# Spreading products of a decoder kernel put on 64 rows of TensorE each, instead of 128

## The chip, the cores and the metric

The kernel runs on one core of one Trainium2 chip. The metric is the device time of one execution in microseconds, as the median of several runs; lower is better. Each engine of the core (TensorE, VectorE, ScalarE, GpSimd, SyncE) runs its own list of instructions in order, and waits on semaphores that the others raise.

## The reference

Six sublayers of a pre-norm decoder are computed on 64 sequences of 128 tokens with 256 channels, each added to the running x. Two of them are attention layers with 16 heads of 16 channels and a softmax over all 128 keys; the mask of keys is in the first alone:

```python
x = x + _L0_attn_ref(_layernorm(x), ...)                       # attention in a window of 7 tokens
x = x + _L0_xattn_ref(_layernorm(x), ctx, ctx, mask, Wp, bp)   # tag "b" in the kernel
x = x + _L0_ffn_ref(_layernorm(x), ...)                        # slots and a gated unit
x = x + _L1_attn_ref(_layernorm(x), ...)                       # causal, with a position bias, tag "1"
x = x + _L1_xattn_ref(_layernorm(x), ctx, ...)                 # tag "x"
x = x + _L1_ffn_ref(_layernorm(x), ...)                        # quantized, with a convolution, tag "g"

# in _L0_xattn_ref
score = jnp.einsum('bhqd,bhkd->bhqk', q, k) / jnp.sqrt(jnp.float32(DK))
score = jnp.where(sm == 0, jnp.float32(-1000000000.0), score)
p_attn = jax.nn.softmax(score, axis=-1) * sm
# in _L1_xattn_ref
scores = jnp.einsum('bhqd,bhkd->bhqk', q, k)
attn = jax.nn.softmax(scores, axis=-1)
```

## The kernel before

The 64 sequences are worked on two at a time (B = 2). Four such pairs are in work at once: they are the four chains, and each chain has two of the eight PSUM banks (`c.ps[:, 0, :]` and `c.ps[:, 1, :]`, 128 partitions of 512 float32 each) and its own tiles in SBUF. A chain makes eight turns, each of them all six sublayers for two sequences, so there are 32 turns of a chain in all. What is interleaved with what is written out by hand: the strings in `ORDER` say for each engine from which chain its next step comes, a step being the code up to the next `yield`. These strings are the lists, and they are the same before and after the change.

Scores are made in two ways in the attention layers "b" and "x". First `scores` (line 1202) makes them with queries on the partitions, for one of two sequences and one half of the heads at a time, and VectorE takes the maximum over the keys (line 696). GpSimd splits each maximum into three bfloat16 parts (`split_pool`, into the tile `m3`), TensorE turns these over (line 1244), and ScalarE copies them to the tile `mT` (line 1004). Then `softmax_tensor` makes the scores a second time, with keys on the partitions (line 1258), and in the same PSUM bank a product ahead of them (line 1254) adds the maxima: its weights `pick` hold ones in the three rows of one head group, 32 rows of the partitions to each group, and zeros elsewhere, so that it spreads the maxima of that group over all 128 keys. ScalarE takes the exponential out of the banks (line 1013), and TensorE multiplies it with the values (line 1221).

In "b" the maxima must leave masked keys out. For this `scores` puts another product ahead of its own (line 1208), whose weights `first` are ones in one row and zero elsewhere, and whose other operand is the tile `mask_bf`, which holds the mask of the keys (0 or -2^30) in the same way on all 128 partitions.

The products of the scores themselves (lines 1212 and 1258) contract over 64 rows: rows 0 to 63 go to bank 0, rows 64 to 127 to bank 1, four products of 256 columns for each bank, and the two banks by turns. The products at lines 1208 and 1254 contract over all 128 rows, one product of 512 columns for each bank. Index `2 * i + o` of `pick` has its ones in rows 32 * (2 * i + o) to 32 * (2 * i + o) + 2, so for bank 0 they lie in rows 0 to 63 and for bank 1 in rows 64 to 127. A pair of these products is issued 256 times at line 1254 (32 turns of a chain, two layers, four each) and 128 times at line 1208 (32 turns, one layer, four each). Line 1317 uses `pick` as well, on 128 rows, and isn't touched.

Of the kernel before, what the change touches and what calls it, by code (L numbers as in the profile page):

```python
# [14 lines left out]
NSEQ, T, D = 64, 128, 256  # L15
# [16 lines left out]
GROUPS = 4  # L32
PER = H // GROUPS
# [166 lines left out]
def spread(ap, dim, n):  # L200
    ap = ap.unsqueeze(dim)
    shape = list(ap.shape)
    shape[dim] = n
    return ap.broadcast_to(shape)
# [423 lines left out]
def flat(tile):  # L628

    inner = " ".join("abcde"[:len(tile.shape) - 1])  # L630
    return tile.rearrange(f"p {inner} -> p ({inner})")
# [570 lines left out]
def scores(e, c, k, v, masked=False):  # L1202

    t, b, x = c.t, v // 2, v % 2
    mm = [None, None]
    if masked:
        for i in range(2):
            e.matmul(c.ps[:, i, :], k["first"][:], spread(t["mask_bf"][:, T * b:T * b + T], 1, PER), start=True, stop=False)
    for j in range(KT):
        for i in range(2):  # L1210
            p = slice(64 * i, 64 * i + 64)
            mm[i] = e.matmul(c.ps[:, i, 2 * T * j:2 * T * j + 2 * T], t["qh"][p, j, x, b, :], flat(t["kx"][p, j, b]), start=not masked,  # L1212
                             stop=not masked or j == KT - 1)
    return mm


def heads_tensor(e, c, b, r, out, p):

    for a in range(PER):
        h = 8 * (a // 2) + 2 * r + a % 2  # L1220
        mm = e.matmul(out[32 * a:32 * a + 32, :], c.t["va"][:, b, VH * h:VH * h + 32], p(a), start=True, stop=True)  # L1221
    return mm


def softmax_tensor(e, c, n, tag, k, masked=False):

    t, ps, act, dve, pool, done = c.t, c.ps, c.act.of(n), c.dve.of(n), c.pool.of(n), c.pe.now
    e.wait_ge(*act(f"{tag}_k"))
    if masked:
        e.wait_ge(*pool("c_mask"))  # L1230
    else:
        e.wait_ge(*act(f"{tag}_v"))
    for v in range(2 * B):
        if v:
            e.wait_ge(*dve(f"{tag}_mx{2 * v - 1}"))
        for i, mm in enumerate(scores(e, c, k, v, masked)):
            mm.then_inc(*done(f"{tag}_s{2 * v + i}"))
        yield
    half = ps[:, 0, :].bitcast(BF16)
    e.wait_ge(*pool(f"{tag}_m3"))  # L1240
    for b in range(B):
        for a in range(PER):
            c0 = T * (PER * b + a)
            mm = e.transpose(half[:, c0:c0 + T], t["m3"][:, b, a].rearrange("p r s -> p (r s)"), k["ident_bf"][:])
    mm.then_inc(*done(f"{tag}_mT"))
    yield
    for u in range(2 * B):
        b, o = u // 2, u % 2
        if u == 0:
            e.wait_ge(*act(f"{tag}_mT"))  # L1250
        else:
            e.wait_ge(*act(f"{tag}_ex{u - 1}" if o else f"{tag}_ou{b - 1}"))
        for i in range(2):
            e.matmul(ps[:, i, :], k["pick"][:, 2 * i + o, :], flat(t["mT"][:, b]), start=True, stop=False)  # L1254
        for j in range(KT):
            for i in range(2):
                p = slice(64 * i, 64 * i + 64)
                mm = e.matmul(ps[:, i, 2 * T * j:2 * T * j + 2 * T], t["kx"][p, j, b, o, :], t["qh"][p, j, :, b, :], start=False,  # L1258
                              stop=j == KT - 1)
        mm.then_inc(*done(f"{tag}_t{u}"))  # L1260
        yield
        if o:
            e.wait_ge(*act(f"{tag}_ex{u}"))
            for r in range(GROUPS):
                mm = heads_tensor(e, c, b, r, ps[:, 0, T * r:T * r + T], lambda a: t["p"][:, a % 2, r // 2, 2 * (a // 2) + r % 2, :])
            mm.then_inc(*done(f"{tag}_u{b}"))
            yield


def causal_tensor(e, c, n, tag, k):  # L1270

    t, ps, act, dve, done = c.t, c.ps, c.act.of(n), c.dve.of(n), c.pe.now
    e.wait_ge(*act(f"{tag}_k"))
    e.wait_ge(*act(f"{tag}_v"))
    for v in range(2 * B):
        if v:
            e.wait_ge(*act(f"{tag}_ou{v - 1}"))
        for i, mm in enumerate(scores(e, c, k, v)):
            mm.then_inc(*done(f"{tag}_s{2 * v + i}"))
        yield  # L1280
        for u in (2 * v, 2 * v + 1):
            e.wait_ge(*act(f"{tag}_ex{u}"))
            for a in range(PER):
                mm = e.transpose(ps[:, u % 2, T * a:T * a + T], t["s"][:, u % 4, a, :], k["ident"][:])  # L1284
            mm.then_inc(*done(f"{tag}_pT{u}"))
            yield
        e.wait_ge(*act(f"{tag}_pc{2 * v + 1}"))
        for i in range(2):
            mm = heads_tensor(e, c, v // 2, 2 * i + v % 2, ps[:, 0, T * i:T * i + T], lambda a: t[f"pT{i}"][:, a, :])
        mm.then_inc(*done(f"{tag}_u{v}"))  # L1290
        yield
# [181 lines left out]
def tensor_turn(e, c, n, k):  # L1473
# [13 lines left out]
    yield from flipped_tensor(e, c, n, "b", k, 0)  # L1487
    e.wait_ge(*c.dve.of(n)("a_y"))
    yield from softmax_tensor(e, c, n, "b", k, masked=True)
    yield from outputs_tensor(e, c, n, "b", k, k["wpT"])  # L1490
    yield from flipped_tensor(e, c, n, "f", k, 0)
# [8 lines left out]
    e.wait_ge(*c.dve.of(n)("1_y"))  # L1500
    yield from projections_tensor(e, c, n, "x", k, k["wqkvxT"], "ctxT")
    yield from softmax_tensor(e, c, n, "x", k)
    yield from outputs_tensor(e, c, n, "x", k, k["woxT"], 3)
    yield from mlp_tensor(e, c, n, k)
# [213 lines left out]
def shape_constants():  # L1718
    p = np.arange(128)
    f = np.float32  # L1720
    expand = np.zeros((4, 3, 8, 4, 128), f)
    for b in range(4):
        for r in range(128):
            expand[b, :, r // DH, b, r] = 1
    head_sum = np.zeros((128, KT, 32), f)
    for j in range(KT):
        head_sum[p, j, 8 * j + p // DH] = 1
    s = 32 * (p[:, None] // 32) + np.arange(32)[None, :]
    return {
        "ident": np.eye(128, dtype=f),  # L1730
        "parity": np.stack([(p % 32 < 16), (p % 32 >= 16)], 1).astype(f),
        "head_sum": head_sum.reshape(128, KT * 32),
        "expand": expand.reshape(96, 4 * 128),
        "half": np.stack([(p % 64 < 32) * 0.25, (p % 64 >= 32) * 0.25], 1).astype(f),
        "rows_of": np.stack([(p // 32 == i) & (p % 32 < 3) for i in range(GROUPS)] + [p == 0], 1).astype(f),
        "third": np.stack([p % 32 == i for i in range(3)], 1).astype(f),
        "causal": np.where(p[None, :] > p[:, None], f(-CAUSAL), f(0)),
        "keys": s.astype(f),
        "pos": np.tile(p.astype(f), (128, 1)),
        "pos7": np.repeat(np.linspace(0.0, 1.0, WIN, dtype=f), H)[:, None],  # L1740
        "of_window": np.repeat(np.eye(WIN, dtype=f), H, 0),
        "of_head": np.tile(np.eye(H, dtype=f), (WIN, 1)),
        "diag16": np.tile(np.eye(H, dtype=f)[:, None, :], (1, WIN, 1)),
    }
# [59 lines left out]
```

## Time and profile before

| | |
|---|---|
| median of 3 runs | 3364.3 us (3353.72 to 3367.71) |
| profiled execution | 3359.88 us |
| its span, first to last instruction | 3358.1 us |
| TensorE matmuls (PE) busy | 2939.3 us |
| TensorE weight loads (PEld) busy | 2077.8 us |
| VectorE (DVE) busy | 2527.9 us |
| ScalarE (ACT) busy | 2180.8 us |
| GpSimd (POOL) busy | 753.5 us |
| mean granted clock of TensorE, share of full speed | 0.962 |

The profile is of one execution. Busy time of an engine is the time in which at least one of its instructions runs, so two matmuls that run side by side count once. PE stands for matmuls, PEld for weight loads, which run beside them. The end of a matmul is modelled, and the next one starts before it; the distance from start to start is what a matmul costs. A few matmul records are missing: line 1254 has 385 of its 512. A name such as `chain_arena` is the large tile of a chain of which `qh`, `kx`, `p` and others are parts; `chain_xn` at line 1254 is the tile that holds `mT`.

### The profile page before, as it was taken

How to read it: one execution, taken by the hardware profiler on the slowest of the kernel's cores; microseconds unless marked ns; L12 is line 12 of the kernel's file. 1: busy time of each engine (PE TensorE's matmuls, PEld its weight loads, DVE VectorE, ACT ScalarE, POOL GpSimd, SP SyncE). 2: the span in 40 equal slices, each digit the busy share in tenths (PEclk: the TensorE clock that was granted, in tenths of full speed). 3: DMA queues.
4: the chain of work that ended last, by engine and by line, in shares of the span. 5: the costliest groups of instructions: out<-in, count | busy, mean ns of one | idle time of the engine just before them, and what ended most of it. 6: DMA issues, size and time to landing. Idle time of an engine off the chain costs nothing.

```text
span 3358.1 us, 59674 instructions
## 1 busy us (share of the span) xinstructions
PE 2939.3 (88%) x23279; PEld 2077.8 (62%) x23406; DVE 2527.9 (75%) x5446; ACT 2180.8 (65%) x4271; POOL 753.5 (22%) x1360
## 2 busy tenths in 40 slices
PE   3799986999879998899988998899988998889984
PEld 3556754666656766567655666567665676556763
DVE  6846598756897579975897768976798758887676
ACT  2258763577646876577855777657765677557773
POOL 1420013300232112320133102321032301232000
PEclk8899997999999999999999999999999999999996
DMA  4000010000000000000000000000000000000000
GB/s 154 1 1 1 4 26 16 1 1 5 23 12 9 1 15 12 20 1 1 15 23 9 1 4 16 20 9 1 5 22 15 6 1 15 12 20 1 1 1 13
DMA packets 43467, 43.47 MB, mean 13 GB/s; under 512 B 8576, under 2 KB 41184, under 8 KB 43184
## 3 DMA queue, kind: packets, MB, share of 16 engines
q1 hardware_dynamic: 41200, 36.46, 3.7%
q8 instruction: 184, 3.01, 0.4%
q10 hardware_dynamic: 1984, 3.18, 0.3%
q14 instruction: 99, 0.81, 0.1%
HBM read 31.24 MB, written 8.39 MB: 12 GB/s over the span
## 4 chain that ended last, share of the span: by engine, by line
PE 59%; DVE 23%; ACT 9%; issue 4%; POOL 3%; DMA 1%; SPq 0%; DVEq 0%; POOLq 0%; ACTq 0%
PE banks L1179 9%; PE banks L1212 9%; PE banks L1258 6%; PE banks L1320 4%; PE banks L1221 4%; DVE chain_m L696 4%; PE banks L1197 3%; PE banks L1254 3%; PE banks L1284 3%; DVE chain_arena L890 2%; PE banks L1404 2%; PE banks L1299 2%; DVE chain_arena L774 2%; ACT chain_arena L1013 2%; PE banks L1344 2%
## 5 line engine op out<-in xcount | busy, mean ns | idle before, releaser
L1212 PE MATMUL banks<-chain_arena 64*128 64x256 f32 x3072 | 438.5, 407 | 39.3 <-DVE chain_m L696 28.2
L696 DVE TENSOR_REDUCE chain_m<-banks 128x4 f32<-128x512 f32 x512 | 329.3, 683 | 113.2 <-PE banks L1212 111.5
L1513 POOL TENSOR_SCALAR chain_ng<-chain_sv 128x2 f32<-128x2 f32 x192 | 52.9, 276 | 1448.5 <-DVE chain_sv L677 1448.4
L1212 PEld LDWEIGHTS banks<-chain_arena 64*128 64x128 f32 x3072 | 273.8, 189 | 168.0 <-issue 85.6
L1034 ACT ACTIVATE chain_arena<-chain_arena,chain_m 128x128 f32<-128x128 f32 x1024 | 323.8, 392 | 27.7 <-DVE chain_m L696 25.0
L968 ACT ACTIVATE chain_xn<-chain_xa,chain_nm,chain_rs 128x256 f32<-128x256 f32 x384 | 209.2, 595 | 163.3 <-POOL chain_nm L1517 162.6
L1258 PE MATMUL banks<-chain_arena 64*128 64x256 f32 x2048 | 295.1, 407 | 0.0
L1258 PEld LDWEIGHTS banks<-chain_arena 64*128 64x128 f32 x2048 | 178.7, 188 | 122.7 <-issue 110.6
L692 DVE TENSOR_TENSOR chain_arena<-banks,pos_bias 128x512 f32<-128x512 f32 x256 | 175.1, 684 | 105.4 <-PE banks L1212 105.3
L1221 PE MATMUL banks<-chain_arena,chain_va 128*32 128x128 f32 x5120 | 195.5, 279 | 35.4 <-ACT chain_arena L1013 23.0
L1013 ACT ACTIVATE chain_arena<-banks,chain_mask_k 128x1024 f32<-128x1024 f32 x128 | 142.4, 1113 | 103.3 <-PE banks L1258 102.5
L1567 POOL TENSOR_TENSOR chain_arena<-chain_arena 128x512 f32<-128x512 f32 x128 | 168.8, 1336 | 155.4 <-DVE chain_arena L774 155.2
L1179 PE MATMUL banks<-chain_arena,wqkv0T 128*128 128x256 f32 x768 | 188.7, 392 | 6.3 <-ACT chain_arena L975 6.3
L1013 ACT ACTIVATE chain_arena<-banks 128x1024 f32<-128x1024 f32 x128 | 131.6, 1028 | 95.0 <-PE banks L1258 94.3
L717 DVE TENSOR_TENSOR chain_xa<-banks,chain_xa 128x512 f32<-128x512 f32 x96 | 66.0, 688 | 165.2 <-PE banks L1320 165.1
L1221 PEld LDWEIGHTS banks<-chain_arena,chain_va 128*32 128x32 f32 x5120 | 126.7, 110 | 100.3 <-issue 37.8
L696 DVE TENSOR_REDUCE chain_m<-chain_arena 128x4 f32<-128x512 f32 x256 | 175.7, 686 | 8.8
L1284 PE MATMUL banks<-ident,chain_arena 128*128 128x128 f32 x1024 | 158.3, 281 | 14.2 <-ACT chain_arena L1034 13.6
L774 DVE TENSOR_TENSOR chain_arena<-banks,chain_arena 128x512 f32<-128x512 f32 x224 | 146.7, 683 | 28.8 <-PE banks L1369 19.6
L1254 PE MATMUL banks<-chain_xn,pick 128*128 128x512 bf16 x385 | 127.2, 385 | 45.5 <-ACT chain_arena L1013 20.9
L1179 PEld LDWEIGHTS banks<-chain_arena,wqkv0T 128*128 128x128 f32 x768 | 143.1, 194 | 34.4 <-ACT chain_arena L975 8.2
L1145 ACT ACTIVATE chain_arena<-chain_arena,pack 128x256 f32<-128x256 f32 x256 | 138.5, 595 | 32.6 <-DVE chain_arena L881 32.0
(314 smaller groups left out, 7013.2 us busy)
## 6 DMA issues: line engine op xcount, KB each, us to landing
chain_xn<-in_ctx SPq DMA_DIRECT2D x32, 256.0 KB, 2.8
chain_xa<-in_x SPq DMA_DIRECT2D x32, 256.0 KB, 3.1
out<-chain_xa SPq DMA_DIRECT2D x32, 256.0 KB, 2.2
chain_arena<-in_mask SPq DMA_DIRECT2D x32, 128.0 KB, 3.7
f_w1t<-in_w1t ACTq DMA_DIRECT2D x1, 1024.0 KB, 7.5
f_w2t<-in_w2t ACTq DMA_DIRECT2D x1, 1024.0 KB, 14.7
wqkv0T<-in_wqkv0T ACTq DMA_DIRECT2D x1, 768.0 KB, 17.1
whh<-in_whh SPq DMA_DIRECT2D x1, 768.0 KB, 10.3
```

Source lines behind the costliest of these rows:

```text
L692: e.tensor_tensor(flat(t["s"][:, u % 4]), c.ps[:, u % 2, :], flat(k["pos_bias"][:, r]), ALU.add).then_inc(*done(f"{tag}_bi{u}"))
L696: e.tensor_reduce(m, s.rearrange("p (j o) t -> p j o t", o=2), AX.X, ALU.max, negate=True).then_inc(*done(f"{tag}_mx{u}"))
L774: e.tensor_tensor(halves(ring[:, slot]), bank(c, w % 2), halves(t["vp"])[:, :, w:w + T], ALU.mult).then_inc(*done(f"a_pv{w}"))
L968: e.activation(t["xn"][:, b, :], t["xa"][:, b, :], ACT.Identity, scale=t["rs"][:, b:b + 1], bias=t["nm"][:, b:b + 1]).then_inc(*done(f"{ta ...
L1013: e.activation(flat(t["p"][:, u % 2]), flat(ps), ACT.Exp, bias=t["mask_k"][:, b:b + 1] if masked else 0.0).then_inc(*done(f"{tag}_ex{u}"))
L1034: ex = e.activation(s, s, ACT.Exp, bias=max_of(t["m"], u // GROUPS, row_group(u), a))
L1179: mm = e.matmul(c.ps[:, i, N * m:N * m + N], w[:, j, c0 + 128 * m:c0 + 128 * m + 128], flat(src[:, j]), start=(j == 0), stop=(j == KT - 1))
L1212: mm[i] = e.matmul(c.ps[:, i, 2 * T * j:2 * T * j + 2 * T], t["qh"][p, j, x, b, :], flat(t["kx"][p, j, b]), start=not masked, stop=not mas ...
L1221: mm = e.matmul(out[32 * a:32 * a + 32, :], c.t["va"][:, b, VH * h:VH * h + 32], p(a), start=True, stop=True)
L1254: e.matmul(ps[:, i, :], k["pick"][:, 2 * i + o, :], flat(t["mT"][:, b]), start=True, stop=False)
L1258: mm = e.matmul(ps[:, i, 2 * T * j:2 * T * j + 2 * T], t["kx"][p, j, b, o, :], t["qh"][p, j, :, b, :], start=False, stop=j == KT - 1)
L1284: mm = e.transpose(ps[:, u % 2, T * a:T * a + T], t["s"][:, u % 4, a, :], k["ident"][:])
```

## The change

The two spreading products of each pair take half of the rows each: the one for bank 0 contracts over rows 0 to 63, the one for bank 1 over rows 64 to 127. So that `first` has a one in each half, its row mask is changed from partition 0 to partitions 0 and 64. Nothing else changes: the number of instructions, their order, their waits and the tiles are as before.

```diff
     if masked:
         for i in range(2):
-            e.matmul(c.ps[:, i, :], k["first"][:], spread(t["mask_bf"][:, T * b:T * b + T], 1, PER), start=True, stop=False)
+            p = slice(64 * i, 64 * i + 64)
+            e.matmul(c.ps[:, i, :], k["first"][p], spread(t["mask_bf"][p, T * b:T * b + T], 1, PER), start=True, stop=False)
...
         for i in range(2):
-            e.matmul(ps[:, i, :], k["pick"][:, 2 * i + o, :], flat(t["mT"][:, b]), start=True, stop=False)
+            p = slice(64 * i, 64 * i + 64)
+            e.matmul(ps[:, i, :], k["pick"][p, 2 * i + o, :], flat(t["mT"][p, b]), start=True, stop=False)
...
-        "rows_of": np.stack([(p // 32 == i) & (p % 32 < 3) for i in range(GROUPS)] + [p == 0], 1).astype(f),
+        "rows_of": np.stack([(p // 32 == i) & (p % 32 < 3) for i in range(GROUPS)] + [p % 64 == 0], 1).astype(f),
```

## Rows read from the trace of the kernel before

**Rows 1.** Page, part 1: busy time of each engine, share of the span, instructions.
```profile
PE 2939.3 (88%) x23279; PEld 2077.8 (62%) x23406; DVE 2527.9 (75%) x5446; ACT 2180.8 (65%) x4271; POOL 753.5 (22%) x1360
```

**Rows 2.** Windows: stretch, its length, busy time of each engine (instructions), granted clock, DMA.
```profile
1721.00:1754.00 33.00, 30.50 (x299) 19.41 (x301) 29.05 (x54) 17.83 (x25) 6.13 (x10) 1.00 0.07 21
1754.00:1787.00 33.00, 26.74 (x175) 17.88 (x177) 29.71 (x66) 20.21 (x37) 17.04 (x24) 0.90 0.03 9
...
1853.00:1886.00 33.00, 29.63 (x266) 20.10 (x269) 27.94 (x70) 19.80 (x44) 9.56 (x15) 1.00 0.00 1
...
1919.00:1952.00 33.00, 32.90 (x303) 24.74 (x304) 15.91 (x33) 25.47 (x54) 3.34 (x10) 1.00 0.01 1
...
sum 396.00, PE 359.95 PEld 255.41 DVE 308.41 ACT 269.51 POOL 93.75; mean PE 30.00 PEld 21.28 DVE 25.70 ACT 22.46 POOL 7.81
```

**Rows 3.** Page, part 4: the chain that ended last, by engine and by line.
```profile
PE 59%; DVE 23%; ACT 9%; issue 4%; POOL 3%; DMA 1%; SPq 0%; DVEq 0%; POOLq 0%; ACTq 0%
PE banks L1179 9%; PE banks L1212 9%; PE banks L1258 6%; PE banks L1320 4%; PE banks L1221 4%; DVE chain_m L696 4%; PE banks L1197 3%; PE banks L1254 3%; PE banks L1284 3%; DVE chain_arena L890 2%; PE banks L1404 2%; PE banks L1299 2%; DVE chain_arena L774 2%; ACT chain_arena L1013 2%; PE banks L1344 2%
```

**Rows 4.** Lines, shapes apart: operation, shapes, count, busy us, mean ns, idle before.
```profile
L1212 PE MATMUL banks<-chain_arena 64*128 64x256 f32 x3072 | 438.5, 407 | 39.3 <-DVE chain_m L696 28.2 <-ACT chain_arena L1044 5.9 <-ACT chain_va L996 3.9
L1258 PE MATMUL banks<-chain_arena 64*128 64x256 f32 x2048 | 295.1, 407 | 0.0
...
L1254 PE MATMUL banks<-chain_xn,pick 128*128 128x512 bf16 x385 | 127.2, 385 | 45.5 <-ACT chain_arena L1013 20.9 <-ACT chain_arena L1017 8.7 <-ACT chain_xn L1004 8.1
...
L1208 PE MATMUL banks<-chain_mask_bf,first 128*128 128x512 bf16 x256 | 80.6, 398 | 28.2 <-DVE chain_m L696 22.3 <-issue 5.7
```

**Rows 5.** Timeline, matmuls: start, us to the modelled end, line, shapes, count.
```profile
1725.84 0.61 PE L1254 MATMUL banks<-chain_xn,pick 128*128 128x512 bf16 x2
1726.38 1.13 PE L1258 MATMUL banks<-chain_arena 64*128 64x256 f32 x8
1727.44 0.61 PE L1208 MATMUL banks<-chain_mask_bf,first 128*128 128x512 bf16 x2
1727.98 1.14 PE L1212 MATMUL banks<-chain_arena 64*128 64x256 f32 x8
1729.05 0.43 PE L1221 MATMUL banks<-chain_arena,chain_va 128*32 128x128 f32 x8
```

**Rows 6.** Timeline, weight loads of the same stretch, with the idle time before them.
```profile
1725.84 0.11 PEld L1254 LDWEIGHTS banks<-chain_xn,pick 128*128 128x128 bf16 x2 [0.41 <-issue]
1726.38 0.73 PEld L1258 LDWEIGHTS banks<-chain_arena 64*128 64x128 f32 x8 [0.42 <-issue]
```

**Rows 7.** Timeline, matmuls, where one group on 64 rows follows another.
```profile
378.21 1.13 PE L1258 MATMUL banks<-chain_arena 64*128 64x256 f32 x8
379.18 1.03 PE L1212 MATMUL banks<-chain_arena 64*128 64x256 f32 x8
380.14 0.66 PE L1284 MATMUL banks<-ident,chain_arena 128*128 128x128 f32 x4
```

**Rows 8.** Source line 1254: what ended idle time before it (us, times).
```profile
  ACT chain_arena L1013: 54.8, 71
...
  ACT chain_arena L1017: 18.0, 23
  ACT chain_xn L1004: 17.9, 34
```

**Rows 9.** Source line 1208: the same.
```profile
  DVE chain_m L696: 53.0, 52
```

**Rows 10.** Waits: engine and line, for whom, us in total, times, longest.
```profile
ACT chain_arena L1013 <- PE banks L1258: 196.8, 148, 3.7
...
DVE chain_m L696 <- PE banks L1212: 111.5, 83, 7.1
```

**Rows 11.** Windows, columns as in rows 2: an early and a middle stretch of 400 us.
```profile
150.00:550.00 400.00, 344.53 (x2689) 240.02 (x2704) 274.13 (x596) 254.60 (x507) 74.74 (x145) 0.93 0.03 7
...
1350.00:1750.00 400.00, 363.92 (x2972) 259.33 (x2991) 317.86 (x687) 274.14 (x538) 93.83 (x168) 0.99 0.04 11
```

## The prediction

> **What bounds the kernel now.** I read the page first. Matmuls fill 88% of the span, VectorE 75%, ScalarE 65% [rows 1]. The chain that ended last spends 59% of its length on matmuls and 23% on VectorE, and the lines that this change touches or follows stand high in it: 9% line 1212, 6% line 1258, 3% line 1254 [rows 3]. Then I cut one turn of the four chains (396 us of the middle, twelve slices of 33 us) into windows [rows 2]: TensorE is busy for 359.95 of the 396 us, but not evenly. From 1919 to 1952 it is full (32.90 of 33) and VectorE is half idle (15.91); from 1754 to 1787 VectorE has 29.71 and TensorE 26.74. So TensorE is the bound for most of a turn, and VectorE has a part of its own. Last I looked at single groups of matmuls from start to start, which shows what a pair costs.
>
> **What a pair costs now.** From the start of the pair at line 1254 to the first product of the scores pass 1726.38 - 1725.84 = 0.54 us, and 0.54 as well at line 1208 [rows 5]. The eight products of the scores on 64 rows take 1.06 from their start to the next group's (1726.38 to 1727.44, and 1.07 from 1727.98 to 1729.05). Together: 1.60. What is in it?
> - Two products on 64 rows that go to different halves run side by side: eight of them, busy for 438.5 us x3072 at a mean of 407 ns each [rows 4], where 3072 x 0.407 one after another would be 1250. So a pair of halves costs about what a single product costs.
> - A change between a group on 64 rows and a group on all rows costs time. Where line 1212 follows line 1258, both on 64 rows, the start-to-start time of the first group is 379.18 - 378.21 = 0.97, against 1.06 where a group on full rows follows [rows 5, 7]. That is 0.09 for the change. The group that follows then takes 380.14 - 379.18 = 0.96 though it does end in such a change; its modelled length is 1.03 in place of 1.13 [rows 7]. So another 0.10 is the weight load of its first pair, which is exposed after a change and hidden without one. The loads show this too: before line 1258 the load engine is idle for 0.42 us with nothing to wait for [rows 6].
> - Of the 0.54, 0.09 is thus the change, and 0.45 two products of 512 columns one after another, about 0.22 each.
>
> **What the change does to it.**
> - The second product of a pair runs beside the first: 0.22 saved. Nothing in this trace shows a 64-row product of 512 bfloat16 columns. Bounds: nothing saved, if it doesn't overlap (as two products on full rows do now, [rows 5]); 0.22 if it does as the float32 halves do. I take 0.22: the nearest rows are those of the same banks, the same halves and the same alternation [rows 4, 7].
> - The change of rows between pair and scores goes: 0.09 saved. The load of the scores' first weights goes under the pair: 0.10 saved. Bounds for this load: 0 to 0.10. I take 0.10, since rows 7 show it hidden behind a group on the same halves, float32 behind float32; here it is float32 behind bfloat16.
> - So 0.54 + 1.06 = 1.60 becomes 0.22 + 0.96 = 1.18, and 0.42 is saved, where TensorE waited before the pair: the change of rows is then made while it is idle. That holds for 71 + 23 + 34 = 128 pairs at line 1254 [rows 8] and 52 at line 1208 [rows 9], 180 of 384.
> - In the other 204 the change of rows moves ahead of the pair. Behind a group on full rows it now costs 0.09 there, and 0.33 is left. Behind a group on 64 rows a change goes that was paid before, and 0.51 is saved. Behind groups on a part of the columns (lines 1221 and 1344), which I expect to cost a change in both kernels, it is 0.42. Most have full rows ahead; I take 0.38 for the mix. The pair's own weight load could be exposed there by up to the same 0.10; the two bfloat16 loads take 0.11 together [rows 6] and delay their products hardly at all now, so I take 0.
> - Sum: 180 x 0.42 + 204 x 0.38 = 75.6 + 77.5 = 153 us of TensorE's time, from 384 x 0.11 = 42 (no overlap in the pair, and a change paid at entry: 0.42 - 0.22 - 0.09) to 384 x 0.51 = 196.
> - `first` has one more row of ones and the mask is read from both halves: no instruction more or less, so 0. No wait, transfer or step is added or moved.
>
> The Trainium skill ("TensorE: Matmul & The Clock Gate", Part 3, what overlaps and what doesn't) says that a weight load runs beside matmuls in flight only if its row group is another one. By this the scores' first loads would stay exposed, and the sum would be 153 - 38 = 115. The trace speaks against it: in rows 7 the second group uses the same rows, and its load costs nothing that shows.
>
> **From TensorE's time to the end.** 153 us is what the end could move at most by my sum, if TensorE were always the bound. Two readings for the share:
> - By the chain: line 1254 is in it with 3% of 3358, about 100 us, of 127.2 that it is busy; line 1212 with 9%, about 302 of 438.5; line 1258 with 6%, about 201 of 295.1 [rows 3, 4]. So 0.68 to 0.79, about 0.7: 107 us. That is before another path takes the chain's place.
> - By slices: of the four in rows 2 that from 1919 is TensorE's alone (share near 1), that from 1754 VectorE's (near 0), and in those from 1721 and 1853 the two stand side by side (about a half each). That makes 0.5.
> I take 0.6, between the two: the chain counts what lies on it and not the path that comes next, and the slices weigh four of twelve alike. 0.6 x 153 = 92. From the profiled execution, 3359.88 - 92 = 3268. The median of the runs is 4.4 above that execution, so 3272.
>
> What is freed is passed on at once: ScalarE waits 196.8 us for line 1258 and VectorE 111.5 for line 1212 [rows 10]. Both are released earlier by what the pair saves.
>
> **The rivals.**
> - *VectorE takes over.* The order of steps is fixed, and where VectorE is the fuller engine TensorE's gain turns into waiting for it. If nothing counts in half of the slices and a half in the rest, a quarter of 153 is left: 38 us, 3326. For it: VectorE at 29.05 and 29.71 of 33 us [rows 2]. Against: over a turn it has 396 - 308 = 88 us of slack and TensorE 36, and the cut is 153 / 8 = 19 us per turn. Chance 0.14.
> - *The pair doesn't overlap, or the loads stay exposed.* The pair costs 0.45 as now and only the change of rows moves: between 42 and 384 x 0.20 = 77 us of TensorE's time, about 60, times 0.6 = 36: 3328. For it: no row has such a product. Against: rows 4 and 7. Chance 0.06.
> - *Slower, by the clock.* TensorE with less to do could be granted the lower of its two levels more often. In the middle of the run the granted clock is 0.99 of its 2.4 GHz level, in the early stretch, with 344.53 us busy of 400, it is 0.93 [rows 11]. A fall of the seven stretches after the first from 0.99 to 0.91 would lengthen 363.92 us to 395.9, 32 us each, 224 in all, of which 0.6 count: 134, against 92 won: slower by 42, 3406. It decides from about 0.93 on (363.92 x 0.06 / 0.93 = 23.5; x 7 x 0.6 = 99). Against: with the cut TensorE is still at about 345 of 385 us, 0.90. Chance 0.03. The Trainium skill (the same page, Part 1) has the clock follow how busy TensorE was lately, which points to this side and gives it no price here.
> - *Nothing moves*, because the fixed order spends all that is freed in waits: within 17 us of before. Chance 0.05.
>
> **How the numbers follow.** My forecast has the remaining 0.72. Its own spread comes from the share (0.4 to 1.0) and the sum (115 to 165): 46 to 165 us won, most of it 55 to 140. The range holds this and most of the first two rivals: 3228 to 3322. What a measurement of this kernel can tell from no change is about 0.5%, 17 us. Faster by more: 0.72 + 0.13 + 0.06 = 0.91; within: 0.06; slower: 0.03.
>
> **What would show it.** In the profile after, the group of line 1254 reads 64*128 64x512 bf16, two of them last about 0.39 together in place of 0.61, and 0.22 pass to the scores behind them; the scores' eight last 1.03 and not 1.13, and the idle time of the load engine before lines 1212 and 1258 that nothing explains gets smaller. Matmuls' busy time falls from 2939 to about 2790. The granted clock stays at 0.95 or more. VectorE's and ScalarE's busy times stay, their shares rise, and ScalarE waits less for line 1258. It is wrong if 0.45 pass from the pair to the scores (no overlap), if the scores' eight still take 1.13 (load not hidden), or if busy time falls as said but the span by less than 50 us (VectorE or the order took over).

## The result and the profile after

The change makes the kernel faster: 3284.83 us median (3283.72 to 3287.36, 4 runs) against 3363.92 us (3353.72 to 3367.71, 4 runs), a ratio of 0.9771 with a 95% interval of 0.9748 to 0.9793, or 79 us. Timed again later, in five rounds beside the kernel before: 3284.91 against 3360.2, ratio 0.9774 (0.9755 to 0.9793). The forecast was 3272, in a range of 3228 to 3322: the sign and what was expected inside TensorE held, and the gain is 13 us smaller than the 92 forecast.

Line numbers move by one at line 1208 (now 1209) and 1212 (now 1213), and by two from 1254 on (1256, 1260). The page of the kernel after, parts 1 and 4, answers to [rows 1, 3]:

```profile
PE 2836.4 (86%) x23406; PEld 2073.9 (63%) x23406; DVE 2522.0 (77%) x5446; ACT 2178.7 (66%) x4271; POOL 755.3 (23%) x1360
...
PE 49%; DVE 31%; ACT 11%; POOL 4%; issue 4%; DMA 1%; SPq 0%; DVEq 0%; POOLq 0%; ACTq 0%
PE banks L1179 8%; PE banks L1213 7%; DVE chain_m L696 5%; PE banks L1322 4%; PE banks L1222 4%; PE banks L1260 4%; PE banks L1197 3%; DVE chain_arena L890 3%; PE banks L1286 2%; DVE chain_arena L927 2%; PE banks L1406 2%; DVE chain_arena L730 2%; DVE chain_arena L931 2%; DVE chain_stat L674 2%; DVE chain_arena L774 2%
```

Matmuls are busy for 103 us less, and the span is only 76 us shorter (3358.1 to 3282.0). In the chain that ended last, matmuls fall from 59% to 49% and VectorE rises from 23% to 31%.

The groups that answer to [rows 4], by line with shapes apart:

```profile
L1213 PE MATMUL banks<-chain_arena 64*128 64x256 f32 x3072 | 426.2, 399 | 42.4 <-DVE chain_m L696 28.1 <-ACT chain_va L996 7.5 <-ACT chain_arena L1044 5.9
L1260 PE MATMUL banks<-chain_arena 64*128 64x256 f32 x2048 | 268.2, 382 | 0.0
...
L1256 PE MATMUL banks<-chain_xn,pick 64*128 64x512 bf16 x512 | 100.9, 391 | 34.9 <-ACT chain_arena L1013 22.9 <-ACT chain_arena L1017 6.0 <-ACT chain_xn L1004 5.7
...
L1209 PE MATMUL banks<-chain_mask_bf,first 64*128 64x512 bf16 x256 | 52.4, 406 | 28.7 <-DVE chain_m L696 22.8 <-issue 5.7
```

The timeline of matmuls after the change, which answers to [rows 5] (start, us to the modelled end):

```profile
1687.24 0.39 PE L1256 MATMUL banks<-chain_xn,pick 64*128 64x512 bf16 x2
1687.47 1.03 PE L1260 MATMUL banks<-chain_arena 64*128 64x256 f32 x8
1688.33 0.38 PE L1209 MATMUL banks<-chain_mask_bf,first 64*128 64x512 bf16 x2
1688.55 1.03 PE L1213 MATMUL banks<-chain_arena 64*128 64x256 f32 x8
...
1691.42 0.39 PE L1256 MATMUL banks<-chain_xn,pick 64*128 64x512 bf16 x2
1691.65 1.03 PE L1260 MATMUL banks<-chain_arena 64*128 64x256 f32 x8
...
1693.22 1.03 PE L1213 MATMUL banks<-chain_arena 64*128 64x256 f32 x8
1694.18 1.08 PE L1222 MATMUL banks<-chain_arena,chain_va 128*32 128x128 f32 x32
```

A pair now passes to the scores after 0.23 or 0.22 us where it took 0.54; the eight products of the scores last 1.03 and not 1.13; and they reach a group of another shape after 0.96 (1693.22 to 1694.18), or a pair of another chain, on the same halves, after 0.86 (1687.47 to 1688.33).

The weight loads of the same stretch, which answer to [rows 6]:

```profile
1687.24 0.10 PEld L1256 LDWEIGHTS banks<-chain_xn,pick 64*128 64x128 bf16 x2 [0.33 <-issue]
1687.25 0.85 PEld L1260 LDWEIGHTS banks<-chain_arena 64*128 64x128 f32 x8
1688.12 0.10 PEld L1209 LDWEIGHTS banks<-chain_mask_bf,first 64*128 64x128 bf16 x2
1688.34 0.84 PEld L1213 LDWEIGHTS banks<-chain_arena 64*128 64x128 f32 x8
```

The scores' first loads start 0.01 us behind the pair's and run under it. The idle time of 0.42 us that stood before them is gone there, and one of 0.33 stands before the pair: the change of rows (between a group on 64 rows and one on all 128) has moved to the entry.

### The profile page after: what moved, and what is told of

The parts are those of the page before. It is cut to its first block, busy times and chain, and to the rows that moved or that the text cites. A ratio compares the mean times of both kernels' runs of the same rounds, so it can differ in the third digit from the quotient of the medians.

```text
span 3282.0 us, 59801 instructions
## 1 busy us (share of the span) xinstructions
PE 2836.4 (86%) x23406; PEld 2073.9 (63%) x23406; DVE 2522.0 (77%) x5446; ACT 2178.7 (66%) x4271; POOL 755.3 (23%) x1360
## 4 chain that ended last, share of the span: by engine, by line
PE 49%; DVE 31%; ACT 11%; POOL 4%; issue 4%; DMA 1%; SPq 0%; DVEq 0%; POOLq 0%; ACTq 0%
PE banks L1179 8%; PE banks L1213 7%; DVE chain_m L696 5%; PE banks L1322 4%; PE banks L1222 4%; PE banks L1260 4%; PE banks L1197 3%; DVE chain_arena L890 3%; PE banks L1286 2%; DVE chain_arena L927 2%; PE banks L1406 2%; DVE chain_arena L730 2%; DVE chain_arena L931 2%; DVE chain_stat L674 2%; DVE chain_arena L774 2%
## 5 line engine op out<-in xcount | busy, mean ns | idle before, releaser
L1213 PE MATMUL banks<-chain_arena 64*128 64x256 f32 x3072 | 426.2, 399 | 42.4 <-DVE chain_m L696 28.1
L1213 PEld LDWEIGHTS banks<-chain_arena 64*128 64x128 f32 x3072 | 286.0, 191 | 119.9 <-DVE chain_m L696 41.2
L1260 PE MATMUL banks<-chain_arena 64*128 64x256 f32 x2048 | 268.2, 382 | 0.0
L1260 PEld LDWEIGHTS banks<-chain_arena 64*128 64x128 f32 x2048 | 200.5, 192 | 23.5
L1286 PEld LDWEIGHTS banks<-ident,chain_arena 128*128 128x128 f32 x1024 | 116.0, 141 | 68.3 <-ACT chain_arena L1034 29.8
```

## The experiments

Each was timed in turn with the kernel before; "after" is the change.

**One half of the change at a time.** Only the maxima's pairs on halves (256 of 384), an edit of the kernel before, in which `first` keeps its single row of ones:

```diff
-            e.matmul(ps[:, i, :], k["pick"][:, 2 * i + o, :], flat(t["mT"][:, b]), start=True, stop=False)
+            p = slice(64 * i, 64 * i + 64)
+            e.matmul(ps[:, i, :], k["pick"][p, 2 * i + o, :], flat(t["mT"][p, b]), start=True, stop=False)
```

> Only the products that spread the maxima (256 of the 384 pairs) work on halves; the mask's stay on 128 rows. Theory A (every pair is worth the same, about 0.2 us of the end): 79 x 2/3 = 53 us under before, about 3311. Rival B (the mask's pairs stand where TensorE is full and the others where it waits): under 40 us, over 3324.

Only the mask's pairs (128), an edit of the kernel after, which puts the maxima's back on 128 rows:

```diff
-            p = slice(64 * i, 64 * i + 64)
-            e.matmul(ps[:, i, :], k["pick"][p, 2 * i + o, :], flat(t["mT"][p, b]), start=True, stop=False)
+            e.matmul(ps[:, i, :], k["pick"][:, 2 * i + o, :], flat(t["mT"][:, b]), start=True, stop=False)
```

> Only the mask's products (128 pairs) work on halves. Theory A: 79 / 3 = 26 us under before, about 3338. Rival B: 40 us or more, 3324 or less. If the two alone sum to well under 79, a part of the gain needs both.

Measured: 3299.69 us, ratio 0.9828 (0.9805 to 0.9851), 62 us under before; and 3336.49, ratio 0.9927 (0.9912 to 0.9942), 25 us under. That is 0.24 and 0.20 us for each pair, and 87 in all against 79 for both: the two halves add up within their intervals, and theory A holds against rival B. Where a pair stands matters little.

**Less and more of the same work.** Each pair issued twice, on halves (shown for the maxima's; the mask's are doubled in the same way):

```diff
-        for i in range(2):
+        for r, i in ((0, 0), (0, 1), (1, 0), (1, 1)):
...
-            e.matmul(ps[:, i, :], k["pick"][p, 2 * i + o, :], flat(t["mT"][p, b]), start=True, stop=False)
+            e.matmul(ps[:, i, :], k["pick"][p, 2 * i + o, :], flat(t["mT"][p, b]), start=r == 0, stop=False)
```

> The change, with each pair on halves issued twice (the second adds the same again). It puts 384 x 0.22 = 84 us back on TensorE. Theory A: 40 to 50 us over after, about 3330. Rival C: VectorE hides most of it, under 25 us over after.

Measured: 3314.27 us (3312.8 to 3314.48), 29 us over after, at a median clock of 0.963 for 0.955. The timeline shows that the second pair does cost 0.22: from pair to scores pass 0.44 us (1704.80 to 1705.24).

```profile
1704.80 0.60 PE L1256 MATMUL banks<-chain_xn,pick 64*128 64x512 bf16 x4
1705.24 1.03 PE L1260 MATMUL banks<-chain_arena 64*128 64x256 f32 x8
```

So, if the sum of 153 us is right, the first 153 - 84 = 69 us taken from TensorE moved the end by 3361.53 - 3314.27 = 47 (0.68 of it), and the next 84 by 29 (0.35). The truth lies between theory A and rival C: what a saved microsecond is worth falls as more is saved. A part of this fall goes with the clock, as is worked out below.

No pair at all (shown for the maxima's; the mask's are left out in the same way):

```diff
-        for i in range(2):
-            p = slice(64 * i, 64 * i + 64)
-            e.matmul(ps[:, i, :], k["pick"][p, 2 * i + o, :], flat(t["mT"][p, b]), start=True, stop=False)
...
-                mm = e.matmul(ps[:, i, 2 * T * j:2 * T * j + 2 * T], t["kx"][p, j, b, o, :], t["qh"][p, j, :, b, :], start=False,
-                              stop=j == KT - 1)
+                mm = e.matmul(ps[:, i, 2 * T * j:2 * T * j + 2 * T], t["kx"][p, j, b, o, :], t["qh"][p, j, :, b, :], start=True, stop=True)
```

> The change, and then neither spreading product is issued at all (masks and maxima are left out of the scores). It frees 384 x 0.22 = 84 us more of TensorE's time. Theory A (about half of what TensorE saves moves the end, here too): 40 to 50 us under after, about 3240. Rival C (VectorE is the bound from here on): under 20 us, over 3265.

Measured: 3278.77 us (3275.9 to 3286.91), 6 under after. These 6 are not clear of noise: the intervals of the two ratios to before, 0.9742 to 0.9772 and 0.9748 to 0.9793, overlap. The 84 us of the expectation were wrong. The timeline of this kernel (columns as above; lines 1252 and 1209 are the scores here) shows why:

```profile
1686.33 1.14 PE L1252 MATMUL banks<-chain_arena 64*128 64x256 f32 x8
...
1687.90 1.13 PE L1209 MATMUL banks<-chain_arena 64*128 64x256 f32 x8 [0.44 <-DVE chain_m L696]
1688.97 1.08 PE L1217 MATMUL banks<-chain_arena,chain_va 128*32 128x128 f32 x32
```

Without a pair ahead the scores' first loads stand open again: 1687.90 to 1688.97 is 1.07 where it was 0.96. A pair on halves costs 0.225 and hides 0.10, so leaving it out frees 0.12 and not 0.22, about 384 x 0.12 = 46 us in all. Of these 46 some 6 came out at the end, which fits rival C's size, though not its cause, as the next runs show.

**VectorE relieved.** In both kernels, and without pairs, the reductions for the maxima read half of the keys (the other half is left out):

```diff
-        e.tensor_reduce(m, s.rearrange("p (j o) t -> p j o t", o=2), AX.X, ALU.max, negate=True).then_inc(*done(f"{tag}_mx{u}"))
+        e.tensor_reduce(m, s.rearrange("p (j o) t -> p j o t", o=2)[:, :, :, 0:T // 2], AX.X, ALU.max, negate=True).then_inc(*done(f"{tag}_mx{u}"))
```

> The change, with VectorE relieved: the 768 reductions for the maxima read 64 of the 128 keys (the other half is left out), about 0.34 us less each, 33 us per turn. Theory A (TensorE is the bound in most places and both count in part): some 60 to 120 us under after. Rival C (VectorE is the bound after the change): over 150 us under after.

> The kernel before, with VectorE relieved in the same way. Theory A': what VectorE takes of the gain shows as a difference between this and the run before it in the list: with VectorE relieved the change should be worth more than 79 us, about 110 to 130 of its 153. Rival D (VectorE has no part in it, the rest is lost to the clock or to the other engines' waits): the difference stays at 75 to 85 us.

> No spreading products at all (left out, as before in the list), and VectorE relieved by half of the keys. Against the run with the pairs on halves and VectorE relieved it frees 84 us of TensorE's time. Theory A': with VectorE relieved 0.7 to 0.85 of it moves the end, 60 to 70 us. Rival D: the same share as with VectorE at its full work.

Measured: after 3237.61 us (3230.62 to 3243.0), before 3316.91 (3314.61 to 3317.16), no pairs 3228.57 (3223.76 to 3229.8). Parts 1 and 4 of the page of the change with VectorE relieved:

```profile
PE 2821.3 (87%) x23406; PEld 2065.6 (64%) x23406; DVE 2330.8 (72%) x5446; ACT 2171.0 (67%) x4271; POOL 751.2 (23%) x1360
...
PE 53%; DVE 22%; ACT 15%; POOL 5%; issue 4%; DMA 1%; SPq 0%; DVEq 0%; POOLq 0%; ACTq 0%
```

VectorE has 191 us less to do (2522.0 to 2330.8), and the change is worth 3316.91 - 3237.61 = 79.3 us with it, as it was without (79.1); each of the two is known to about 7 or 8 us. Leaving the pairs out gives 9 more, where it gave 6. So theory A', which asked for 110 to 130, is refuted and rival D holds: as far as VectorE was relieved here, its load did not hold the gain back, though its share of the chain had gone from 23% to 31% with the change. The relief itself brings 43 us before and 47 after, so VectorE does have a part in the time of both kernels, but less than theory A's 60 to 120 and far from the 150 that a VectorE bound would give.

**The clock.** Ten products that nobody reads, in all 32 turns, ahead of TensorE's wait for the window weights:

```diff
     half = ps[:, 1, :].bitcast(BF16)
+    for i in range(10):
+        e.matmul(ps[:, 1, :], k["ident_bf"][:], k["w1t"][:, 0:512], start=True, stop=True)
     e.wait_ge(*dve("a_f3"))
```

> The change, and ten products of 512 columns that nobody reads ahead of TensorE's wait for the window weights (line 1357), where it was idle for 2.6 us in a middle turn before its clock fell. Theory E (the falls of the clock cost what the gain lacks): the granted clock rises above 0.955 and the time falls by 5 to 15 us. Rival: the products cost what the clock gives back or more, the time is the same or up to 20 us longer.

Measured: 3319.46 us, 35 over after, at a clock of 0.960 for 0.955. They add 32 x 10 x 0.22 = 70 us to TensorE's order, and half of it reached the end; what the clock gave back was less. Theory E's number missed, and so did its rival's (up to 20 us longer). Then I looked for the turns in which the idle time is really there. In the kernel after, in chain 3 alone, TensorE waits 2.6 us at the window weights and 3.05 at the normalized input of layer f, once a turn each, and in the middle turns the clock falls 2 to 3 us behind each. The second of them in the timeline after:

```profile
1740.92 0.93 PE L1170 MATMUL banks<-ident,chain_xn 128*128 128x128 f32 x4 [3.05 <-ACT chain_xn L968]
```

Fillings in these twelve places, in the change, in the kernel before and without pairs:

```diff
+WARM = {"a": 9, "f": 11}
...
+def keep_warm(e, c, n, tag, k, i):
+
+    if c.index == 3 and n >= (3 if tag == "f" else 1):
+        for _ in range(WARM[tag]):
+            e.matmul(c.ps[:, i, :], k["ident_bf"][:], k["w1t"][:, 0:512], start=True, stop=True)
...
+    if tag == "f":
+        keep_warm(e, c, n, tag, k, i)
     for b in range(B):
         e.wait_ge(*act(f"{tag}_xn{b}"))
...
+    keep_warm(e, c, n, "a", k, 1)
     e.wait_ge(*dve("a_f3"))
```

> The change, and idle time of TensorE filled with products that nobody reads in twelve places alone: chain 3, seven turns at the wait for the window weights (nine products of 512 columns, idle 2.6 us there) and five at the normalized input of layer f (eleven, idle 3.04 us); in the middle turns the granted clock fell about 2 us behind each. Theory E (what the clock loses between before and after, some 18 us of TensorE's time, is lacking at the end): granted clock 0.960 or more and 8 to 25 us less than after. Rival F (what the clock costs lies beside waits): the clock rises and the time stays within 5 us of after.

> The same twelve fillings in the kernel before. Theory E: it loses less to the clock (0.962), so it gains less, 0 to 12 us, and the change is then worth over 85 us between the two filled kernels. Rival F: both move by the same amount, and the difference stays at 79.

> No spreading products (masks and maxima left out of the scores) with the same fillings. Without them TensorE's order is only 0.12 us per pair shorter than after the change, since the first loads of the scores are exposed again: 48 us, of which 6 reached the end, at a clock of 0.949. Theory E: with the clock held up it comes 15 us or more under the run with the pairs and the fillings. Rival F: under 10.

The same place in the filled change (line 1182 is the former 1170):

```profile
1741.92 2.32 PE L1170 MATMUL banks<-w1t,ident_bf 128*128 128x512 bf16 x10
1744.91 0.93 PE L1182 MATMUL banks<-ident,chain_xn 128*128 128x128 f32 x4 [0.67 <-ACT chain_xn L968]
```

Measured: the filled change 3276.0 us (3272.53 to 3279.05), clock 0.959, ratio 0.9746 (0.9723 to 0.977); the filled kernel before 3344.66 (3339.49 to 3351.88), clock 0.968, ratio 0.9955 (0.9941 to 0.9969). So filling is worth 17 us before (10 to 20 by the interval of its ratio). Between the filled kernels the change is worth 69 us, give or take 9. That is not theory E's 85 or more, and it lies at the edge of F's 79. But the two runs don't show that the clock has no part in the difference, because the fillings didn't bring the two clocks together: by the medians of the runs it rose from 0.962 to 0.969 in the kernel before, and only from 0.955 (0.957 in the run further below) to 0.960 in the change. The gap between the kernels grew from at most 0.007 to nearly 0.010, and the gain got smaller.

Without pairs the filled kernel takes 3282.71 us (3265.01 to 3291.64) at a median of 0.950: its clock wasn't held up (median 0.9475 without the fillings). The places were chosen by another kernel's trace; that this is why was not tested, and the run says nothing on the theories.

**The change once more,** unaltered, beside before:

> The change itself once more, beside the kernel before in five rounds, since the filled version (ratio 0.9746 to before) and the change (0.9771) were timed in different sets of runs. If the fillings of idle time are worth 8 us, the ratio here is 0.976 to 0.979 and the time near 3285; if they are worth nothing, it is 0.973 to 0.976, near 3277.

Measured: 3284.91 us (3282.05 to 3288.55), 0.9774 (0.9755 to 0.9793). So the filled change is probably the fastest version with all its work done, by 9 us. All its runs lie under all of the change's, but the intervals of the two ratios overlap, and they weren't timed on the same chip.

**What the clock costs, from the scatter.** The executions with a clock on record (100, in 17 sets of one kernel in one round) differ among themselves: in one set of 16 executions the kernel before takes from 3343.66 us at a clock of 0.967 to 3368.8 at 0.960. A line fitted within all sets gives 2.3 us for each 0.001 of the clock (standard error 0.2). This is an estimate and no experiment: what lowers the clock of an execution may lengthen it by other ways too. By it the clock that the change loses (0.962 to 0.955, in the second timing 0.961 to 0.957) costs 9 to 16 us, and without that loss the gain would be 84 to 95 us, 0.55 to 0.62 of 153. The same correction turns the 0.68 of the first 69 us into 0.62, the 0.35 of the next 84 into 0.5 to 0.56, and the 0.13 of the last 46 into 0.5 to 0.6 (the clock falls to 0.9475 there). By this estimate most of the fall in what a saved microsecond is worth goes with the clock. With VectorE relieved the clock's gap was 0.009 (0.9655 to 0.9565), which hides 5 to 12 us more of the change's worth than without the relief, still far from the 31 to 51 more that theory A' asked for.

## Why the prediction was right, point by point

- *What a pair costs before, and that it overlaps on halves:* right. 0.22 was taken without a row for a 64-row product of 512 bfloat16 columns; it is 0.22 to 0.23. The rival without overlap is refuted.
- *The load goes under the pair:* right, 1.13 became 1.03. In the kernel after, the load at 1687.25 runs beside the pair of 1687.24 on the same rows. The rule of the Trainium skill by which this shouldn't happen ("TensorE: Matmul & The Clock Gate", Part 3, what overlaps and what doesn't) is contradicted by the trace. Part 2 of the same page of the Trainium skill, on loading the stationary operand, allows it when the load goes to a background buffer. The trace agrees in its times (0.01 us from load to load, 0.22 from pair to scores); it doesn't show which buffer was written.
- *The change of rows moves to the entry:* right, with its price. In the kernel before, where line 1179 came ahead without a wait and no record is missing, the pair started 0.216 us behind the last of its products, as closely as these follow each other; in the kernel after it starts 0.311 behind, 0.095 more for the 0.09 forecast, and the load engine idles 0.33 us before line 1256. Behind lines 1222 and 1346 the distance stayed (0.205 and 0.31), as expected.
- *The 180 pairs behind a wait:* misread. The counts of rows 8 and 9 take in idle spells of the matmuls and of the weight loads, which often belong to the same pair. For matmuls alone they come to 22 + 27 + 11 + 13 = 73 pairs in the kernel before (us, times, longest, below). The forecast's own prices then give 73 x 0.42 + 311 x 0.38 = 149 us and not 153, so the slip changes little.

```profile
PE banks L1208 <- DVE chain_m L696: 22.3, 22, 2.1
...
PE banks L1254 <- ACT chain_arena L1013: 20.9, 27, 1.3
...
PE banks L1254 <- ACT chain_arena L1017: 8.7, 11, 1.1
PE banks L1254 <- ACT chain_xn L1004: 8.1, 13, 1.5
```

- *The sum of 153 us of TensorE's time:* not measured as such, but it closes. Busy time fell by 103. In the kernel before 127 first products of pairs are missing from the records, 0.22 us each, so its true busy time was 28 higher. And TensorE spends longer at the lower of its two levels: 2 x (1 - 0.955) x 3282 = 295 us against 2 x (1 - 0.962) x 3358 = 255, 40 more, half of which, at about 0.88 busy, is 18 us of work stretched. 103 + 28 + 18 = 149, an estimate that fits the sum of 149 to 153.
- *The share of 0.6, and the clock at nothing:* one of these two terms was off. Without a term for the clock the share was too large: it was 76 / 153 = 0.50. With one of 9 to 16 us, by the estimate from the scatter, a share of 0.55 to 0.62 is left, and the 0.6 stands. Which of the two it was, the runs don't decide. In the forecast's terms: of 153 us, 18 went into the clock by the sum above, and TensorE waits longer: it stands idle for 3282.0 - 2836.4 = 445.6 us against 418.8, and with the 28 us of missing records in the latter the rise is 55. 153 - 18 - 55 = 80, for 76. The chain's 0.7 was right for the first part of the cut (0.68 for the first 69 us) and too high for the rest (0.35 for the next 84), as measured with the clock's loss in it.
- *VectorE as the path that takes over:* the reason given for a share under 0.7 is not borne out. The gain was the same 79 us with VectorE relieved by 191. That the range and the number came out near is thus in part luck: the discount came near in size and was argued from the wrong path. The waits that grew are spread over all of TensorE's partners: of its longest waits after (us, times, longest) none is more than 5 us longer than before.

```profile
PE banks L1170 <- ACT chain_xn L968: 28.2, 25, 3.0
...
PE banks L1222 <- ACT chain_arena L1013: 27.4, 47, 2.3
PE banks L1362 <- DVE chain_fw L768: 24.3, 14, 3.1
```

They were 25.1, 23.0 and 21.3 in the kernel before. Between ScalarE, GpSimd and the fixed order of steps, which of them holds the rest back wasn't tried; a new order was not run. How much of the clock's 18 us reached the end stays open too; the estimate from the scatter says 9 to 16.
- *What would show it:* the shapes, the 0.39 for two, the 1.03 and the clock of at least 0.95 came as written. Busy time is 2836 and not 2790, since the forecast forgot that the missing records hide 28 us of it and gave the clock nothing. ScalarE's wait for these scores fell from 196.8 [rows 10] to 134.5 us:

```profile
ACT chain_arena L1013 <- PE banks L1260: 134.5, 123, 3.0
...
DVE chain_m L696 <- PE banks L1213: 84.2, 62, 6.7
```

- *Slower by the clock:* the clock did fall, from 0.962 to 0.955, but not near the 0.93 at which it would have decided, and the kernel got faster.

## What to carry to other kernels

A helper product next to products on halves of the rows should work on halves too, each half for its own bank: two run in the time of one, the change of rows between them goes, and their weight loads hide the next ones'. Read the worth of such an edit from start to start in the timeline, then take the chain's share for the first percent or two of the span and less for what comes behind. In this kernel, the only one measured, it was 0.7 and then half of that, with the fall of the clock in it; so give the clock a term of its own. Before putting the missing part down to the next engine in the chain, relieve that engine in both kernels: if the change is worth the same, it wasn't that engine, at least as far as it was relieved.

## What the runs showed of the hardware that was not expected

- Leaving a product out can free half of what it costs: a pair of 0.225 us hid 0.10 us of weight loads behind it, and without it the scores' group took 1.07 in place of 0.96.
- On halves, fewer products came with a lower clock: 0.963 with the pairs twice, 0.955 with them once, 0.949 without; the kernel before had 0.962. Twelve fillings of idle times of 2.6 to 3 us took 17 us (0.5%) off the kernel before.
